# Step two of a two-step graph attention kernel: sums above the threshold made by GpSimd, and the kept tile behind the second weighing and the row maximum

## The reference, cut to what matters

```python
def _adj_from_feats(Xa, W1, W2, W3):
    logits = (Xa @ W1) @ W2 @ (Xa @ W3).T
    idx = jnp.argsort(-logits, axis=1)
    vals = jnp.take_along_axis(logits, idx, axis=1)
    csum = jnp.cumsum(jax.nn.softmax(vals, axis=1), axis=1)
    k_i = jnp.sum(csum < 0.9, axis=1) + 1
    ...                                   # keep the k_i largest of each row
    return jax.nn.softmax(masked, axis=1)
...
for s in range(2):
    A = _adj_from_feats(Xa, W1, W2, W3)
    Xf = Rf @ Xf
    Xb = Rb @ Xb
    Xa = A @ Xa
    Z = Z + (Xf @ U1[s] + Xb @ U2[s] + Xa @ U3[s])
```

## Time and profile before

| what | value |
|---|---|
| median of 3 runs | 2369.52 us (2368.68 to 2369.74) |
| the profiled execution's own time | 2369.85 us |
| its span | 2368.1 us |
| busy: TensorE, VectorE, ScalarE, GpSimd | 91%, 87%, 82%, 31% |
| chain that ended last | VectorE 46%, TensorE 22%, ScalarE 17%, issue 6%, GpSimd 5% |

### The profile page before, as it was taken

How to read it: one execution, slowest core, us unless ns; L and a number is a source line. 1 busy time by engine, 2 the same in 40 slices (tenths; PEclk the granted TensorE clock), 3 DMA queues, 4 the chain that set the end, 5 groups by cost and what they waited for, 6 DMA issues and landing times.

```text
span 2368.1 us, 26066 instructions
## 1 busy us (share of the span) xinstructions
PE 2154.2 (91%) x8250; PEld 1380.8 (58%) x8250; DVE 2057.3 (87%) x3825; ACT 1939.9 (82%) x2849; POOL 731.0 (31%) x987
## 2 busy tenths in 40 slices
PE   7599999999999998899799999999999999999975
PEld 4377767776777767443355555555555555555454
DVE  5699999999999998134989999999999999999995
ACT  5899999999999995236578988988989889889834
POOL 2133443344333442001123223233232232332332
PEclk9699999999999999999899999999999999999997
DMA  7245444555445452332222112112121221121242
GB/s 245 82 112 131 110 106 100 123 116 115 94 112 122 110 110 52 102 98 41 46 61 55 39 50 57 37 51 55 51 43 50 51 57 36 50 57 40 53 116 70
DMA packets 85166, 190.03 MB, mean 80 GB/s; under 512 B 12193, under 2 KB 65056, under 8 KB 85024
## 3 DMA queue, kind: packets, MB, share of 16 engines
q0 software_dynamic: 26208, 61.37, 16.5%
q1 hardware_dynamic: 56496, 125.48, 16.0%
q10 hardware_dynamic: 2320, 1.48, 0.2%
HBM read 154.19 MB, written 34.10 MB: 80 GB/s over the span
## 4 chain that ended last, share of the span: by engine, by line
DVE 46%; PE 22%; ACT 17%; issue 6%; POOL 5%; DMA 0%; SPq 0%; DVEq 0%; ACTq 0%; POOLq 0%
DVE junk L1869 16%; PE bank L1144 10%; ACT junk L1431 6%; DVE logits L2036 6%; DVE small L1913 4%; DVE logits L1905 4%; DVE small L1811 4%; POOL small L1700 3%; DVE small L1796 3%; PE bank L1118 2%; PE bank L1134 2%; PE bank L753 2%; ACT logits L1324 2%; ACT junk L1390 2%; PE bank L776 2%
## 5 line engine op out<-in xcount | busy, mean ns | idle before, releaser
L1869 DVE SCALAR_TENSOR_TENSOR junk<-logits,small,expd 128x3327 uint8<-128x3327 f32 x184 | 677.9, 3684 | 4.8
L1118 PE MATMUL bank<-both,pair 128*128 128x512 f32 x1352 | 612.8, 598 | 26.4 <-ACT sides L1474 25.4
L1144 PE MATMUL bank<-h_aug,turns 128*128 128x256 f32 x2704 | 634.4, 381 | 1.5 <-ACT turns L1453 1.5
L1144 PEld LDWEIGHTS bank<-h_aug,turns 128*128 128x128 f32 x2704 | 496.6, 190 | 106.5 <-issue 24.9
L1118 PEld LDWEIGHTS bank<-both,pair 128*128 128x128 f32 x1352 | 250.8, 190 | 313.2 <-issue 260.8
L1118 PE MATMUL bank<-h_aug,both 128*128 128x257 f32 x1352 | 335.4, 397 | 29.5 <-ACT sides L1460 28.5
L1118 PEld LDWEIGHTS bank<-h_aug,both 128*128 128x128 f32 x1352 | 258.5, 197 | 112.9 <-ACT sides L1460 48.9
L1684 POOL TENSOR_TENSOR small<-small 128x1 f32<-128x1 f32 x52 | 14.8, 285 | 899.6 <-DVE small L1938 895.5
L1390 ACT ACTIVATE junk<-expd,small 128x3327 int8<-128x3327 f32 x88 | 270.4, 3072 | 3.0 <-POOL small L1679 2.7
L1384 ACT ACTIVATE junk<-expd,small 128x3327 int8<-128x3327 f32 x88 | 270.1, 3069 | 1.5
L1102 PE MATMUL bank<-KTr,QT 64*128 64x512 f32 (+1 forms) x728 | 232.6, 616 | 20.4 <-ACT logits L1324 16.5
(11 more groups left out here) (250 smaller groups left out, 2981.9 us busy)
## 6 DMA issues: line engine op xcount, KB each, us to landing
both<-adj_turned SPq DMA_DIRECT2D x52, 832.0 KB, 6.9
both<-adj_turned POOLq DMA_DIRECT2D x52, 832.0 KB, 11.0
pair<-adj_turned SPq DMA_DIRECT2D x52, 832.0 KB, 4.5
z<-sides POOLq DMA_DIRECT2D x52, 128.0 KB, 3.2
spread<-sides POOLq DMA_DIRECT2D x26, 128.5 KB, 3.7
turns<-spread SPq DMA_DIRECT2D x26, 128.5 KB, 2.1
attended<-att_out SPq DMA_DIRECT2D x26, 128.0 KB, 1.7
expd<-attended SPq DMA_DIRECT2D x26, 128.0 KB, 2.1
```

The source lines that it names most:

```text
L1118: done = pe.matmul(SX[:, 0:width], half(t, h)[:, bass.ts(jj, P)], rows_of(j), start=(j == 0), stop=(j == T - 1))
L1144: last = pe.matmul(AB[:, 0:D], attT[i % 4][:, b, :], h_aug[:, g + b, 0:D], start=(g + b == 0), stop=(g + b == T - 1))
L1869: chain.did(dve.scalar_tensor_tensor(junk[:, 0:N], logits[t % 3][:, 0:N], col(t, "cand"), expd[t % NE][:, 0:N], ALU.is_gt, ALU.mult, accum ...
```

## The change

In step two alone: `sum_larger` on VectorE shrinks to one reciprocal, and GpSimd makes both sums above the threshold itself, with a comparison and a product over 128x24 and five adding steps that fold 24 columns into one. VectorE's order becomes bisect 0, bisect 1, `row_max(t+1)`, `keep(t-1)`, bisect 2 to 4. ScalarE's order becomes: `count_ties(t-1)`, all of `store_logits(t+1)`, `lift(t-1)`, the two checks, `scale_attended(t-2)`, `exponentials(t+1)`, `guess(t+1)`, `turned` 0, 1, 2, the probes with `turned` 3 and 4, 5 between, `turned` 6, `read_sides(t)`. In both steps `keep` takes one reciprocal over two columns where it took two over one; for that, five columns of `small` move. TensorE's and SyncE's orders stay.

```diff
-                            if previous and present:
-                                read_sides(t - 1)
+                            if t == 1:
+                                read_sides(0)
+                            if previous:
                                 count_ties(t - 1)
-                                lift(t - 1)
...
                             if following:
                                 store_logits(t + 1, range(NC))
-                            if t > 1:
-                                scale_attended(t - 2)
+                            if previous and present:
+                                lift(t - 1)
                             if present:
                                 check(t, 0)
                                 check(t, 1)
-                            turned(0)
+                            if t > 1:
+                                scale_attended(t - 2)
                             if following:
                                 exponentials(t + 1)
-                            turned(1, 2)
-                            if following:
                                 guess(t + 1)
-                                probe(t + 1, 0, lambda: turned(3), lambda: turned(4))
-                                probe(t + 1, 1, lambda: turned(5, 6), nothing)
+                                turned(0, 1, 2)
+                                probe(t + 1, 0, lambda: turned(3), nothing)
+                                probe(t + 1, 1, lambda: turned(4, 5), nothing)
+                                turned(6)
...
+                            if present:
+                                read_sides(t)
...
+                    def sum_larger(t):
+                        first_two = small[t % 3][:, 96 + 2 * BEST:96 + 4 * BEST].rearrange("p (n c) -> p n c", n=2)
+                        pool.wait_ge(sem["larger_summed"], t + 1)
+                        chain.did(pool.tensor_scalar(best(t, 2), best(t, 0), col(t, "tau"), None, ALU.is_gt))
+                        chain.wait()
+                        chain.did(pool.tensor_tensor(best(t, 3), best(t, 2), best(t, 0), ALU.mult))
+                        chain.wait()
+                        for w in (12, 6, 3):
+                            chain.did(pool.tensor_tensor(first_two[:, :, 0:w], first_two[:, :, 0:w], first_two[:, :, w:2 * w],
+                                                         ALU.add))
+                            chain.wait()
+                        for n in (1, 2):
+                            chain.did(pool.tensor_tensor(first_two[:, :, 0:1], first_two[:, :, 0:1],
+                                                         first_two[:, :, n:n + 1], ALU.add))
+                            chain.wait()
...
                     def sum_larger(t):
+                        if not first_step:
+                            dve.reciprocal(col(t, "invtau"), col(t, "tau")).then_inc(sem["larger_summed"], 1)
+                            return
...
-                        chain.did(dve.reciprocal(col(t, "invties"), col(t, "ties")))
-                        chain.wait()
-                        chain.did(dve.reciprocal(col(t, "inv"), col(t, "total")))
+                        chain.did(dve.reciprocal(small[t % 3][:, 46:48], small[t % 3][:, 44:46]))
+                        chain.wait()
...
                             bisect(t, 0)
+                            bisect(t, 1)
+                            if following:
+                                row_max(t + 1)
                             if previous:
                                 keep(t - 1)
-                            if following:
-                                row_max(t + 1)
-                            for k in range(1, late):
+                            for k in range(2, late):
                                 bisect(t, k)
```

More of the change, by code:

```diff
@@ L896, in step @@
                 NAMES = ["max", "negmax", "sum", "target", "cand", "mass", "move", "below", "above", "tau",
-                         "invtau", "gt", "have", "need", "count", "n_gt", "ties", "invties", "sharetau", "total", "inv",
-                         "negbig", "less", "half", "halves", "floor", "tail", "side", "limit", "flag", "beyond", "low",
+                         "invtau", "gt", "have", "need", "count", "n_gt", "sharetau", "negbig", "less", "half", "halves", "floor", "tail", "side", "limit", "flag", "beyond", "low",
                          "spare", "over_mean", "var", "log_var", "sigma", "shifted", "least", "most", "hop", "rinv",
-                         "part", "part_up", "negabove", "negtarget", "neglimit"]
+                         "part", "part_up", "negabove", "negtarget", "neglimit", "unused", "ties", "total", "invties", "inv"]
                 PAIRS = ["point0", "point1", "up", "top", "bottom", "d_top", "d_bottom", "high", "deep", "width", "point2"]
+                assert NAMES.index("ties") == 44 and len(NAMES) == 48
                 def col(t, name):
@@ L1680, in prepare @@
                                            ).then_inc(sem["prepared"], 1)
-                    def count_needed(t):
-                        pool.wait_ge(sem["larger_summed"], t + 1)
-                        chain.did(pool.tensor_tensor(col(t, "have"), col(t, "gt"), col(t, "negabove"), ALU.subtract))
-                        chain.did(pool.tensor_scalar(col(t, "beyond"), col(t, "n_gt"), -2.0, float(N), ALU.mult, ALU.add))
-                        chain.wait()
+                    def sum_larger(t):
[13 more added lines that the diff above has]
+                            chain.wait()
+                        chain.did(pool.tensor_tensor(col(t, "have"), best(t, 3)[:, 0:1], col(t, "negabove"),
+                                                     ALU.subtract))
+                        chain.did(pool.tensor_scalar(col(t, "beyond"), best(t, 2)[:, 0:1], -2.0, float(N),
+                                                     ALU.mult, ALU.add))
+                        chain.wait()
@@ new lines, in count_needed @@
+                    def count_needed(t):
+                        if first_step:
+                            pool.wait_ge(sem["larger_summed"], t + 1)
+                            chain.did(pool.tensor_tensor(col(t, "have"), col(t, "gt"), col(t, "negabove"),
+                                                         ALU.subtract))
+                            chain.did(pool.tensor_scalar(col(t, "beyond"), col(t, "n_gt"), -2.0, float(N),
+                                                         ALU.mult, ALU.add))
+                            chain.wait()
+                        else:
+                            sum_larger(t)
```

6 lines of the change are left out of this document (3 added, 3 removed).

## The result

The changed kernel takes 2503.99 us (median of 4 runs, 2503.52 to 2505.78) beside 2369.1 us before: 1.057 times, interval 1.055 to 1.059. 2508 us was forecast.

A forecast was written before the change was run, and what follows sets the result against it. Before, VectorE set the pace, TensorE second; after, a ring through TensorE, logits, maximum and keep. From 2369.85 us: first keep +7.4, 23 iterations +136.2, end -4.7, step one -1, sum 2507.8, forecast 2508 us; range 2485 to 2548.

The forecast's parts named there:

- Step 2: TensorE's wait for `turned` 0, behind exponentials and guess: `multiply` 0 starts at K + 7.3, a new 2.5 us wait.
- K: The end of `keep(t-1)` on VectorE, from which the forecast counted times within a step-two iteration.
- Step 3 to 5: TensorE from `multiply` 0 through `read_sides`, spreads and logits chunks to the last store: K + 7.3 to K + 41.15.
- the walk: One trip in timeline rows from keep through TensorE, logits and maximum to the next keep: 49.3 us, 5.9 more.
- Step 6: VectorE's maximum with two small instructions, keep's preparation, keep and a semaphore behind the last store: 8.13 us.
- The first keep: End of step two's first keep: 1209.3 us before, 1216.7 forecast, +7.4 us.
- step one: The kernel's first step: the merged reciprocal saves 0 to 0.16 us 26 times, taken as -1 us.
- The end: From the last but one keep to the last tile's keep: 76.1 us before, 71.4 forecast, -4.7 us.
- The clock: TensorE's slow clock after idling for keep: 2.65 us lost on turns and spread 3, replacing the `turned` 0 wait; nothing added.
- The rival of two falls an iteration: TensorE's idling before `multiply` 0 brings a second slow stretch: up to 1.6 us an iteration, 2545 us, chance 0.2.
- The ring of VectorE and ScalarE: Search, two bisects, maximum, keep, exponentials to second probe: 44.8 us an iteration; deciding alone, 2404 us, chance 0.04.
- The cross-check: Iteration from TensorE's 42.1 us of work plus 5.0 waiting for keep and 2.5 for `turned` 0: 49.6 us.

The follow-up runs named there:

- orders_alone: The changed kernel with the sums given back to VectorE, keeping both new orders and the merged reciprocal: 2503.8 us, 1.057 times the kernel before.
- keep_and_lift_early: The changed kernel with VectorE's keep ahead of the row maximum and ScalarE's lift ahead of its logits stores again: 2457.5 us, 1.038 times the kernel before.
- turned0_ahead_too: The changed kernel with keep ahead of the maximum, lift ahead of the stores and `turned` 0 ahead of the exponentials: 2396.4 us, 1.011 times the kernel before.
- keep_before_max: The changed kernel with only VectorE's keep put ahead of the row maximum again, ScalarE's order staying new: 2575.6 us, 1.087 times the kernel before.
- without group 2: The changed kernel with TensorE's spread group 2 left out for every tile in step two, sums incomplete: 2500.4 us, executed once.
- sums_alone: The kernel before with only step two's sums above the threshold moved to GpSimd: 2400.1 us, 1.013 times the kernel before.

## Why the prediction was right, point by point

- **The period.** 49.3 forecast, 49.15 measured. Step 2 (`multiply` 0 at K + 7.3): measured 1713.67 - 1706.27 = 7.4. Step 3 to 5: `multiply` 0 to the next maximum, 33.85 by the walk, 1747.30 - 1713.67 = 33.63 measured. Step 6: 8.1 forecast; from 1698.18 to 1706.27, 8.09.
- **The first keep and step one.** +7.4 and -1 forecast, 1214.9 - 1209.3 = +5.6 measured for both. From the start of the search of tile 1 (1193.77, before 1195.64) to the end of the keep it is 21.1 us and was 13.7, the +7.4 of the walk. The mis-sized term is step one, 1.9 us where I took 1. That the merged reciprocal is the cause isn't shown: orders_alone has it too and began this search at 1195.62, and the other runs with the same step one began it between 1190.9 and 1193.3.
- **The end.** 71.4 us from the last but one keep to the last tile's, forecast and measured (2416.69 - 2345.3). That it meets to the tenth is luck. From the end of the last L2067 row to 2416.69 it is 30.4 us, and 29.3 in orders_alone (2387.99 to 2417.32), without GpSimd's seven steps: they cost 1.1 and not 2.1. The forecast's rest, 28.4, was 0.9 too short, which is how much longer VectorE waits for GpSimd there than before (1.93 and 1.01).
- **The sums on GpSimd.** Covered, as forecast. "Uncovered it would cost 2 to 4 us an iteration" was too much: alone they made keep wait 1.3 us longer and cost 1.1 us an iteration.
- **The clock.** Forecast as hidden, and nearly all of it is: the granted clock over 1216 to 1800 us is 0.94, and the slow stretch ends about where `turned` 0 comes. In 18 of 23 iterations `multiply` 0 starts 0.65 us behind the start of `turned` 0, that is, with its end; in 5 the slow spread ends later, and it starts 0.79 to 0.90 behind. That the two ends fall so close together is luck: the forecast took 2.65 us of loss from one fall elsewhere, and here it differs from one iteration to the next. The rival of two falls an iteration did not come. But its price where it is not hidden, 0 to 1.6 us, was too low; 1.4 to 3.1 us was measured in two of the experiments. In keep_and_lift_early all 24 waits of 3.3 to 3.75 us ahead of `multiply` 0 were followed by a loss. By this the trace agrees with the Trainium skill, page "TensorE: Matmul & The Clock Gate", section "HAM oscillation — how this bites in real kernels": a loop with a long wait in every turn pays again in every turn.
- **What the forecast left out.** It checked `turned` 4 (needed at K + 23, there at K + 21) and found no wait, which was right; it did not say that these 2 us bound every gain ahead of that point. The experiments' expectations fell over it. The ring of VectorE and ScalarE, 44.8 by its rows, measured 44.16 in turned0_ahead_too. The cross-check, 49.6, was 0.45 off; it took TensorE's work from a busy time, which is modelled.

## To carry to other kernels

Before a step is moved behind another on one engine, write down what each of the other engines has queued behind its result and whether that queue feeds the step that now stands ahead: here keep waited for a maximum, the maximum for logits, and the logits stood behind the turns that wait for keep. Walk that ring once in timeline rows, and compare it with every other closed path; a loop's pace is that of the longest, and a step's busy time is worth something only where it lies on it. A wait ahead of TensorE on the ring costs its own length and often the slow clock behind it (here up to 3.1 us), so an idle stretch is best put where another wait follows anyway.

## What the runs showed of the hardware that I had not expected

- What TensorE loses behind a wait varies and does not grow in step with the wait. Behind 1.95 us (turned0_ahead_too) it was 1.7 us in three early iterations and nothing from the fifth on; behind 3.24 (keep_before_max) nothing, where 4.35 cost 1.5; behind 3.64 it was 1.4 to 3.05, behind 4.65 1.8 to 3.1. Behind 5.47 us it was 1.35 on the turns and 0.1 to 1.5 on the spread behind them (changed kernel), and the same behind 9.10 (without group 2).
- A GpSimd step on one column per partition lasted 3.5 us when it met a VectorE weighing with two tile operands (1690.39 us in sums_alone), and 0.19 to 0.34 elsewhere; so a chain of 13 such steps is cheap only if it ends before the weighing begins.
